# Two-layer graph network on one core: the Exp table load ahead of tile 0's count copies, an earlier credit, and y's split between the copies of the output weights

## The chip, the cores and the metric

The kernel runs on 1 core of a Trainium2 chip. TensorE (PE in the rows) multiplies into PSUM, VectorE (DVE) and ScalarE (ACT) work between PSUM and SBUF, GpSimd (POOL) only in SBUF, and SyncE (SP) issues most DMAs. Every engine takes its instructions in the order of its own program and waits on semaphores for the others. The metric is the device time of one execution in microseconds (us), lower is better; three executions of the kernel before are given.

## The reference

What is computed, cut to what matters here. N = 1250 nodes of 1024 numbers, 41,250 edges with one of two relations; the second layer's tables of counts come from the same edges.

```
h  = relu(layernorm(x))                       # 1250 x 1024
nx = t5_layer_norm(h, ln_weight)
out = nx @ W_root + bias                      # 1024 -> 286
for r in range(2):                            # relations
    msg  = nx[src] @ W_rel[r] * (edge_type == r)
    sums = segment_sum(msg, dst); cnt = segment_sum(edge_type == r, dst)
    out += sums / max(cnt, 1)
y  = elu(out) @ wo_weight                     # 286 -> 1024, the output weights
x1 = x + h + y
g  = relu(layernorm(x1)); hh = g @ W          # second layer, 1024 -> 1024
e  = exp(-leaky_relu(al[src] + ar[dst], 0.1))
out_x = x1 + elu(segment_sum(e * hh[dst], src) / (segment_sum(e, src) + 1e-5))
```

## The kernel before, in words

The nodes are 10 tiles of 125 rows. The sums over edges are done as dense products: for each tile of target nodes the kernel counts, by matmuls of one-hot rows, how many edges of each relation come from each source node, and multiplies that table of counts by the messages. A tile's counts are made in five groups of 25 target columns. There is no scheduler: the order on each engine is written out by hand, and the engines meet at semaphores.

- **First stage** (0 to 121 us): per tile, normalise, transpose, and multiply by the relation weights; ScalarE copies the result out as `msg_hi` (function `messages`, L545), VectorE writes the self term `root` (L951) and the low part `msg_lo` (L953). All products are done in high and low parts (hi*hi + hi*lo + lo*hi), so each operand exists as a rounded part and a remainder. Among the last tile's products TensorE also counts the five groups of target tile 0 (`windows_counted`, L1406), and ScalarE copies each into `adj0` (L579); five `zero_used` and five `zero_out` signals pace this. Then `back_to_exp` (L582) loads ScalarE's table with Exp and runs one tiny Exp, after which the last tile's `messages` follows.
- **Counting stage** (121 to 243 us): step t counts the groups of tile t (`counted`), copies them out (`counts_evicted`, L602 and L606: a float copy, then a 16-bit copy), multiplies tile t-1's counts by the messages (`summed`, L1502: relation 0 and relation 1 of 20 matmuls each), transposes the summed counts for the second layer in three parts (`turned`, L1526, copied out at L622), and finishes tile t-2: z (`z_of`, L1059 to L1065), its exponential (`elu`, L627), y (`y_of`, L1069 and L1071), its transpose (L1541, L1542), y's split into high and low (`y_split`: L635 on ScalarE, L1077 and L1080 on VectorE), and the output product (`output1`, L1558 to L1561, added to x at L1088). VectorE builds the one-hot rows for the counting (`rows_of`, L973 and L975, about 1.3 us for a group).
- The **output weights** are split once, in step 2: ScalarE copies `wo_hi` for two blocks of 127 rows (L610) and `wo_mix` for the rest (L616), VectorE subtracts (L1050 twice, L1054) and signals `wo_split`. TensorE's `output1(0)` waits for `wo_split` to reach 3, so for all of them; y's low part it needs too, and the middle part of the transposed counts, `turned(1, 1)`, waits for y's split because both use PSUM bank 5:

```
pe.wait_ge(S["yT_lo_rdy"], data(t))
pe.wait_ge(S["wo_split"], len(FK))     # len(FK) is 3
```

- **Credits.** Many semaphores start at 2 so that the first two tiles find their buffers free. VectorE gives `sum_16` its two credits at L1039, in its program behind the last tile's messages and the load of a flag; the first group of a tile's counts is not copied out by ScalarE before `sum_16` allows it (`act.wait_ge(S["sum_16"], room(t))`).
- Both sides of a branch are in the program; the flag says that all edges were found, and in the profiled execution the written-out order of `If_eq(flag, 0)` runs. The other side uses `split_wo` as a whole.
- **Second layer** (243 us to the end): products with W and the attention sums, on TensorE almost without a break.

Of the kernel before, what the change touches and what calls it, by code (L numbers as in the profile page):

```python
# [5 lines left out]
def rgcn_gat_kernel(nc, x, src, dst, edge_type, ln_weight, w_rel, w_root, conv_bias, wo_weight, w_gat, a_gat, out):  # L6

    F32, R32, BF16, F16 = mybir.dt.float32, mybir.dt.float32r, mybir.dt.bfloat16, mybir.dt.float16
    I32, U16 = mybir.dt.int32, mybir.dt.uint16
    ALU, ACT, AX = mybir.AluOpType, mybir.ActivationFunctionType, mybir.AxisListType.X  # L10
# [5 lines left out]
    T = 125  # L16
# [39 lines left out]
    CREDIT = 2  # L56
# [58 lines left out]
    with ctx:  # L115
# [9 lines left out]
        eps = sb(ctx, "eps", [P, 3], F32)  # L125
# [4 lines left out]
        ssq = [sb(ctx, f"ssq{b}", [T, 1], F32) for b in range(2)]  # L130
# [131 lines left out]
        S = {n: sem(n) for n in names}  # L262
# [224 lines left out]
        def _(act):  # L487
            A = nc.scalar
# [85 lines left out]
            messages(1, 1, 0)  # L574
            pads()
            pipeline((transposed, 1), (messages, 2), (normed, -1), steps=(AHEAD, TILES + 1))
            for g in range(NG):
                act.wait_ge(S["zero_used"], g + 1)
                A.copy(adj0[:, :, GW * WD * g:GW * WD * (g + 1)].rearrange("p r (n d) -> p r n d", d=WD), counts_bank(g)).then_inc(S["zero_out"], 1)  # L579

            def back_to_exp():
                A.activation(ssq[0][:], eps[0:T, 0:1], ACT.Exp)  # L582
            back_to_exp()
            messages(TILES - 1, 1, TILES // 2 - 1)
            act.wait_ge(S["zero_out"], NG)
            act.wait_ge(S["table_rdy"], 1)
# [19 lines left out]
                    A.copy(whole(adj_16), whole(adj_hi).bitcast(F32)).then_inc(S["win_16"], 1)  # L606

            def split_wo_of(n):
                    act.wait_ge(S["wo_in"][n], 32)
                    A.copy(wo_hi[:, n, :], wo_raw[:, n, :]).then_inc(S["wo_hi_rdy"], 1)  # L610

            def split_wo():
                split_wo_of(0)
                split_wo_of(1)
                act.wait_ge(S["wo_in"][2], 48)
                A.copy(wo_mix[:], wo_rest[:]).then_inc(S["wo_hi_rdy"], 1)  # L616

            def counts_out(t, b, d, parts=range(3)):
                for c in parts:
# [101 lines left out]
            with act.If_eq(flag, 0):  # L721
                act.wait_ge(S["g_ps"], data(TILES - 1))
                A.copy(ident_16[:], ident[:]).then_inc(S["ident_rdy"], 1)
                act.sem_inc(S["win_out"], NG)
                act.sem_inc(S["win_16"], NG)
                tile = lambda t: (t, t % 2, t // 2)

                def evicted(t, *groups):
                    for g in groups:
                        counts_evicted(t, t % 2, g, True)  # L730

                def turned(t, *parts):
                    counts_out(*tile(t), parts)
                evicted(1, 0, 1)
                turned(0, 0)
                evicted(1, 2)
                turned(0, 1)
                evicted(1, 3)
                turned(0, 2)
                evicted(1, 4)  # L740
                elu(*tile(0))
                evicted(2, 0)
                split_wo()
                evicted(2, 1)
                y_split(*tile(0))
                turned(1, 0)
                evicted(2, 2)
                turned(1, 1)
                evicted(2, 3)
                turned(1, 2)  # L750
                evicted(2, 4)
                elu(*tile(1))
                for t in range(3, TILES):
                    evicted(t, 0)
                    y_split(*tile(t - 2))
                    evicted(t, 1)
                    turned(t - 1, 0)
                    evicted(t, 2)
                    elu(*tile(t - 1))
                    turned(t - 1, 1)  # L760
                    evicted(t, 3)
                    turned(t - 1, 2)
                    evicted(t, 4)
                last = tile(TILES - 1)
                deviation2(0, 0)
                deviation2(1, 1)
                act.wait_ge(S["hot_used"], done(nth(TILES - 1, NG - 1)))
                split_gat_weights(range(0, 1))
                for k in range(1, 4):
                    load_wg(k)  # L770
                y_split(*tile(TILES - 2))
                norm2(0, 0)
                back_to_exp()
                for k in range(4, 6):
                    load_wg(k)
                turned(TILES - 1, 0)
                load_wg(6)
                elu(*last)
                turned(TILES - 1, 1)
                turned(TILES - 1, 2)  # L780
                load_wg(7)
                y_split(*last, yT_hi2)
                transposed2(0, 0, 0)
                norm2(1, 1)
                split_gat_weights(range(1, 5))
                transposed2(1, 1, 0)
                split_gat_weights(range(5, KT))
                second_layer()
# [21 lines left out]
        def _(dve):  # L810
            V = nc.vector
            dve.sem_inc(S["hot_used"], NG)
            dve.sem_inc(S["win_lo"], NG)
            dve.sem_inc(S["x_used"], 1)
            for n in ("bn_rdy", "var_rdy", "rs_rdy", "rstd_rdy", "rms_rdy", "hT_lo_rdy", "g_dve", "deg_rdy", "inv_rdy", "z1_rdy",
                      "zz_rdy", "y_rdy", "yT_lo_rdy", "x1_rdy", "bn2_rdy", "mv2_rdy", "rs2_rdy", "rstd2_rdy", "gT_lo_rdy", "h_dve",
                      "att_u", "att_v", "att_p", "att_lo_rdy", "den_rdy", "rinv_rdy", "logit_rdy"):
                dve.sem_inc(S[n], CREDIT)
# [217 lines left out]
                    dve.wait_ge(S["c_ps"], 3 * room(t))  # L1036
                V.tensor_tensor(columns(adj_lo, b, g), counts_bank(NG * b + g), columns(adj_hi, b, g).bitcast(F32), ALU.subtract).then_inc(S["win_lo"], 1)

            dve.sem_inc(S["sum_16"], CREDIT)  # L1039

            def summed(t, b, d):
                mine = slice(T * b, T * (b + 1))
                dve.wait_ge(S["win_16"], done(nth(t, NG - 1)))
                dve.wait_ge(S["c_ps"], 3 * room1(t))
                V.tensor_tensor(sum_16[:], adj_16[:, 0:TILES, mine], adj_16[:, TILES:BLOCKS, mine], ALU.add).then_inc(S["sum_16"], 1)

            def split_wo():
                for n in range(2):
                    dve.wait_ge(S["wo_hi_rdy"], n + 1)
                    V.tensor_tensor(wo_lo[:, n, :], wo_raw[:, n, :], wo_hi[:, n, :].bitcast(F32),  # L1050
                                    ALU.subtract).then_inc(S["wo_split"], 1)
                dve.wait_ge(S["wo_hi_rdy"], 3)
                middle = slice(FR, 2 * FR)
                V.tensor_tensor(wo_mix[middle, :], wo_rest[middle, :], wo_mix[middle, :].bitcast(F32), ALU.subtract).then_inc(S["wo_split"], 1)  # L1054
# [187 lines left out]
            with dve.If_eq(flag, 0):  # L1242
                tile = lambda t: (t, t % 2, t // 2)

                def rows(t, *groups):
                    if t < TILES:
                        for g in groups:
                            rows_of(nth(t, g))
                dve.wait_ge(S["zero_out"], NG)
                both = adj0[:].bitcast(F32)  # L1250
                V.tensor_tensor(sum_16[:], both[:, 0:TILES], both[:, TILES:BLOCKS], ALU.add).then_inc(S["sum_16"], 1)
                rows(2, 0, 1, 2, 3)
                z_of(*tile(0))
                rows(2, 4)
                y_of(*tile(0))
                summed(*tile(1))
                split_wo()
                y_split(*tile(0))
                rows(3, 0)
                z_of(*tile(1))  # L1260
                y_of(*tile(1))
                rows(3, 1)
                for t in range(3, TILES):
                    summed(*tile(t - 1))
                    rows(t, 2)
                    y_split(*tile(t - 2))
                    output1(*tile(t - 3))
                    rows(t, 3)
                    z_of(*tile(t - 1))
                    rows(t, 4)  # L1270
                    y_of(*tile(t - 1))
                    rows(t + 1, 0, 1)
                last, before = tile(TILES - 1), tile(TILES - 2)
                variance2(0, 0)
                variance2(1, 1)
                summed(*last)
                deviation2(0, 0)
                deviation2(1, 1)
                output1(*tile(TILES - 3))
                y_split(*before)  # L1280
                split_gat_weights(range(0, 1))
                z_of(*last)
                y_of(*last)
                output_half(TILES - 2, 0, 0)
                y_split(*last, yT_hi2, yT_lo2)
                output_half(TILES - 2, 0, 1)
                transposed2(0, 0, 0)
                split_gat_weights(range(1, 5))
                output1(*last)
                split_gat_weights(range(5, 7))  # L1290
                variance2(2, 0)
                split_gat_weights(range(7, KT))
                deviation2(2, 0)
                transposed2(1, 1, 0)
                second_layer()
# [423 lines left out]
```

## Time and profile before

| | us |
|---|---|
| median of 3 runs | 511.51 (510.75 to 511.76) |
| the profiled execution | 510.68 |
| its span | 508.9 |
| TensorE busy | 491.3 (97%) |
| VectorE busy | 374.2 (74%) |
| ScalarE busy | 227.4 (45%) |
| TensorE's waits in 121 to 143 us, by the profile | 0.60, 0.78, 0.52 |

Times in the trace are us from the span's start. The profiled execution is 1.78 us longer than its span. Busy shares are means over stages: in the counting stage the engines follow each other through semaphores every few us, and what bounds it is read from who waited for whom there.

### The profile page before, as it was taken

The numbers are of one execution on the slowest core, as the hardware profiler recorded it, in microseconds if no ns is written. First come the engines' busy times: TensorE is split into PE (matmuls) and PEld (weight loads), VectorE is DVE, ScalarE is ACT, GpSimd is POOL, SyncE is SP. The second block draws the span as 40 slices with busy tenths as digits, with TensorE's granted clock in tenths as the row PEclk, the third lists the DMA queues.
The fourth block names the chain that finished last, engine by engine and source line by source line (L and its number), as shares of the span: only waits on it lengthen the run. The fifth ranks groups of instructions, "written<-read, shape, count | busy, mean of one in ns | idle before, by whom it ended". The sixth has DMA issues, their size and how long they took to land.

```text
span 508.9 us, 7733 instructions
## 1 busy us (share of the span) xinstructions
PE 491.3 (97%) x2953; PEld 422.4 (83%) x2953; DVE 374.2 (74%) x635; ACT 227.4 (45%) x382; POOL 74.9 (15%) x74
## 2 busy tenths in 40 slices
PE   3999999999899999999999999999999999999996
PEld 2889989988889998998788888888888878878785
DVE  4865885599989999997855555556598877777634
ACT  5755543416966666668632222334233323323211
POOL 1182313100000000000000000000083333322400
PEclk9999999999999999999999999999999999999999
DMA  9964264504013334248911111100032232222211
GB/s 254 234 196 129 81 190 127 145 15 114 1 42 109 96 98 147 82 124 300 309 45 42 40 42 43 38 1 0 1 81 82 87 95 62 81 82 81 81 44 44
DMA packets 22186, 49.15 MB, mean 97 GB/s; under 512 B 4798, under 2 KB 10709, under 8 KB 22018
## 3 DMA queue, kind: packets, MB, share of 16 engines
q1 hardware_dynamic: 20879, 44.66, 29.6%
q10 hardware_dynamic: 1008, 3.67, 2.1%
q8 instruction: 26, 0.43, 0.4%
q0 software_dynamic: 256, 0.26, 0.2%
q14 instruction: 17, 0.14, 0.1%
HBM read 33.05 MB, written 16.85 MB: 98 GB/s over the span
## 4 chain that ended last, share of the span: by engine, by line
PE 84%; DVE 7%; DMA 4%; ACT 3%; issue 1%; SPq 0%; ACTq 0%; DVEq 0%
PE ps L1337 11%; PE ps L1605 9%; PE ps L1607 9%; PE ps L1606 9%; PE ps L1502 7%; PE ps L1586 7%; PE ps L1587 7%; PE ps L1588 7%; PE ps L1406 4%; PE ps L1425 2%; DMA xt<-xh_scratch 2%; PE ps L1558 2%; PE ps L1560 1%; PE ps L1559 1%; PE ps L1572 1%; DMA x_scratch<-xt 1%
## 5 line engine op out<-in xcount | busy, mean ns | idle before, releaser
L1605 PE MATMUL ps<-h_hi,att_hi 125*125 125x512 f32 (+1 forms) x190 | 73.6, 387 | 0.0
L1606 PE MATMUL ps<-h_lo,att_hi 125*125 125x512 f32 (+1 forms) x190 | 72.6, 382 | 0.0
L1607 PE MATMUL ps<-h_hi,att_lo 125*125 125x512 f32 (+1 forms) x190 | 72.6, 382 | 0.0
L1586 PE MATMUL ps<-wg,gT_hi 128*125 128x512 f32 x160 | 63.8, 399 | 0.1
L1587 PE MATMUL ps<-wg,gT_hi 128*125 128x512 f32 x160 | 63.1, 395 | 0.0
L1588 PE MATMUL ps<-wg,gT_lo 128*125 128x512 f32 x160 | 63.1, 394 | 0.0
L1502 PE MATMUL ps<-msg_hi,adj_hi 125*125 125x288 f32 x180 | 50.3, 304 | 0.8 <-ACT adj_hi L602 0.8
L1502 PE MATMUL ps<-msg_lo,adj_hi 125*125 125x286 f32 x180 | 45.9, 295 | 0.0
L477 POOL TENSOR_TENSOR some<-first_att 125x625 f32<-125x625 f32 x1 | 2.4, 2441 | 273.3 <-DVE first_att L1162 273.3
L697 ACT ACTIVATE em<-ps,rinv 125x512 f32<-125x512 f32 (+1 forms) x21 | 14.0, 668 | 63.2 <-DVE hp L1208 63.2
L1607 PEld LDWEIGHTS ps<-h_hi,att_lo 125*125 125x125 f32 x190 | 35.3, 186 | 8.0
L1605 PEld LDWEIGHTS ps<-h_hi,att_hi 125*125 125x125 f32 x190 | 35.2, 185 | 7.9
L1606 PEld LDWEIGHTS ps<-h_lo,att_hi 125*125 125x125 f32 x190 | 35.2, 185 | 7.5
L1337 PE MATMUL ps<-w_hi,hT_hi 128*125 128x430 f32 x112 | 40.7, 363 | 0.4 <-DVE hT_lo L928 0.4
L1337 PE MATMUL ps<-w_hi,hT_lo 128*125 128x430 f32 x112 | 40.2, 359 | 0.0
L1337 PE MATMUL ps<-w_lo,hT_hi 128*125 128x430 f32 x112 | 40.0, 357 | 0.0
L1142 DVE CUSTOM_DVE_ANT_0 h_lo<-ps,a_b 125x1024 fp32r<-125x1024 f32 x20 | 24.5, 1224 | 20.0 <-PE ps L1588 19.7
L1586 PEld LDWEIGHTS ps<-wg,gT_hi 128*125 128x125 f32 x160 | 29.7, 186 | 7.5 <-DVE wg L1103 0.5
L1588 PEld LDWEIGHTS ps<-wg,gT_lo 128*125 128x125 f32 x160 | 29.7, 186 | 7.3
L1587 PEld LDWEIGHTS ps<-wg,gT_hi 128*125 128x125 f32 x160 | 29.7, 186 | 6.9
L1502 PEld LDWEIGHTS ps<-msg_hi,adj_hi 125*125 125x125 f32 x180 | 33.4, 186 | 1.2 <-ACT adj_hi L602 1.2
L674 ACT CAST h_hi<-ps 125x1024 fp32r<-125x1024 f32 x10 | 10.1, 1014 | 54.1 <-DVE dot L1142 54.1
(215 smaller groups left out, 1102.3 us busy)
## 6 DMA issues: line engine op xcount, KB each, us to landing
xt<-in_x SPq DMA_DIRECT2D x10, 448.0 KB
xh_scratch<-xt SPq DMA_DIRECT2D x10, 448.0 KB
xt<-xh_scratch SPq DMA_DIRECT2D x10, 448.0 KB
x_scratch<-xt SPq DMA_DIRECT2D x10, 448.0 KB
x1t<-x_scratch SPq DMA_DIRECT2D x10, 448.0 KB
xr<-x_scratch SPq DMA_DIRECT2D x10, 448.0 KB
out_x<-xr SPq DMA_DIRECT2D x19, 224.0 KB
wg_raw<-in_L_gnn_W ACTq DMA_DIRECT2D x7, 512.0 KB, 7.8
```

Source lines behind the costliest of these rows:

```text
L697: A.activation(em[b][:, first:end], heads(b, h, (first, end)), ACT.Exp, scale=rinv[b][:, 0:1]).then_inc(S["el_rdy"], 1)
L1142: V.tensor_tensor_reduce(out=halves(h_lo[:, TILES - 1, :]), in0=hps, in1=halves(a_b[:, s, :]), scale=1.0, scalar=0.0, op0=ALU.mult, op1=AL ...
L1337: last = M.matmul(out, lhsT, rhs, start=(n == 0), stop=(n == len(terms) - 1))
L1406: last = M.matmul(win_bank(n, x), srcs, wide, start=c == 0, stop=c == SLOTS - 1)
L1425: last = M.matmul(bank(2 + 2 * b + n, T, FB), lhsT[b][:, k, :], rhs[:, k, n, :], start=k == 0 and m == 0, stop=k == KT - 1 and m == 2)
L1502: last = M.matmul(*product, start=(s == 0 and n == 0), stop=(end and n == 1), skip_group_check=True)
L1586: M.matmul(to, hi, wg[k][:, 0, cut], start=n == 0, stop=False)
L1587: M.matmul(to, hi, wg[k][:, 1, cut], start=False, stop=False)
L1588: last = M.matmul(to, lo, wg[k][:, 0, cut], start=False, stop=n == KT - 1)
L1605: M.matmul(to, hi[:, s, :], h_hi[:, s, cut], start=s == 0, stop=False)
L1606: M.matmul(to, hi[:, s, :], h_lo[:, s, cut], start=False, stop=False)
L1607: return M.matmul(to, lo[:, s, :], h_hi[:, s, cut], start=False, stop=s == TILES - 1)
```

## The change

Three things change, all around the first two steps of the counting stage.

1. ScalarE: `back_to_exp()` stands ahead of the five copies into `adj0` instead of behind them.
2. VectorE: the two credits of `sum_16` are given at the start of its program, with the others.
3. ScalarE and VectorE, in step 2: the three copies (and subtractions) of the output weights are no longer one piece. On ScalarE the second block follows y's split, and the rest follows the copy of group 2 of tile 2's counts; on VectorE y's split stands behind the first subtraction.

```diff
             pipeline((transposed, 1), (messages, 2), (normed, -1), steps=(AHEAD, TILES + 1))
+            def back_to_exp():
+                A.activation(ssq[0][:], eps[0:T, 0:1], ACT.Exp)
+            back_to_exp()
             for g in range(NG):
                 act.wait_ge(S["zero_used"], g + 1)
                 A.copy(adj0[:, :, GW * WD * g:GW * WD * (g + 1)].rearrange("p r (n d) -> p r n d", d=WD), counts_bank(g)).then_inc(S["zero_out"], 1)
-
-            def back_to_exp():
-                A.activation(ssq[0][:], eps[0:T, 0:1], ACT.Exp)
-            back_to_exp()
             messages(TILES - 1, 1, TILES // 2 - 1)
...
@@ ScalarE, the written-out order
                 evicted(2, 0)
-                split_wo()
+                split_wo_of(0)
                 evicted(2, 1)
                 y_split(*tile(0))
+                split_wo_of(1)
                 turned(1, 0)
                 evicted(2, 2)
+                split_wo_rest()
                 turned(1, 1)
                 evicted(2, 3)
...
@@ VectorE, start of its program
             dve.sem_inc(S["x_used"], 1)
+            dve.sem_inc(S["sum_16"], CREDIT)
...
-            dve.sem_inc(S["sum_16"], CREDIT)
-
...
@@ VectorE, the written-out order
                 summed(*tile(1))
-                split_wo()
+                split_wo_of(0)
                 y_split(*tile(0))
+                split_wo_of(1)
+                split_wo_rest()
                 rows(3, 0)
```

`split_wo_of(n)` and `split_wo_rest()` are the old parts of `split_wo()`, which now calls them in the old order.

ScalarE at the end of the first stage, before (L545 is `messages`, L579 the copies of tile 0's counts, L286 the flag):

```order
L529 CAST hT_hi<-ps 128x500 x2
L545 ACTIVATE msg_hi<-ps,stats 125x2x286
L579 CAST adj<-ps 125x20x25 x5
L582 ACT_TABLE_LOAD
L582 ACTIVATE ssq<-eps 125x1
L545 ACTIVATE msg_hi<-ps,stats 125x2x286
L286 TENSOR_LOAD table
```

and now (line numbers are those of the changed kernel):

```order
L529 CAST hT_hi<-ps 128x500 x2
L545 ACTIVATE msg_hi<-ps,stats 125x2x286
L578 ACT_TABLE_LOAD
L578 ACTIVATE ssq<-eps 125x1
L582 CAST adj<-ps 125x20x25 x5
L545 ACTIVATE msg_hi<-ps,stats 125x2x286
L286 TENSOR_LOAD table
```

The table load and the small Exp moved ahead of the five copies; the last tile's `messages` now follows the fifth copy.

ScalarE in step 2, before (L602 and L606 copy one group of counts, L610 and L616 the output weights, L635 y's split, L622 the transposed counts):

```order
L627 ACTIVATE eb<-zb,eps 125x286
L602 CAST adj_hi<-ps 125x20x25
L606 CAST adj<-adj_hi 125x20x25
L610 CAST wo_hi<-wo_raw 127x1024 x2
L616 CAST wo_mix<-wo_rest 96x1024
L602 CAST adj_hi<-ps 125x20x25
L606 CAST adj<-adj_hi 125x20x25
L635 ACTIVATE yT_hi<-ps 127x125 x2
L635 ACTIVATE yT_hi<-ps 96x125
L622 CAST counts<-ps 125x500
L602 CAST adj_hi<-ps 125x20x25
L606 CAST adj<-adj_hi 125x20x25
```

and now (L601 and L605, L609 and L613, L637, L624 are the same operations):

```order
L601 CAST adj_hi<-ps 125x20x25
L605 CAST adj<-adj_hi 125x20x25
L609 CAST wo_hi<-wo_raw 127x1024
L601 CAST adj_hi<-ps 125x20x25
L605 CAST adj<-adj_hi 125x20x25
L637 ACTIVATE yT_hi<-ps 127x125 x2
L637 ACTIVATE yT_hi<-ps 96x125
L609 CAST wo_hi<-wo_raw 127x1024
L624 CAST counts<-ps 125x500
L601 CAST adj_hi<-ps 125x20x25
L605 CAST adj<-adj_hi 125x20x25
L613 CAST wo_mix<-wo_rest 96x1024
```

y's split moved ahead of two of the three weight copies, and the last of these moved behind three more waits on TensorE's work: group 1, `turned(1, 0)` and group 2 of tile 2.

VectorE in the same step, now (L1048 is the sum of tile 1's counts at its head, L1052 and L1063 the subtractions, L1086 and L1089 y's split, L978 and L980 the one-hot rows of tile 3's group 0, L1068 the start of tile 1's z):

```order
L1048 TENSOR_TENSOR sum<-adj 125x1250
L1052 TENSOR_TENSOR wo_lo<-wo_raw,wo_hi 127x1024
L1086 SCALAR_TENSOR_TENSOR yT_lo<-ps,yT_hi 127x125 x2
L1089 SCALAR_TENSOR_TENSOR yT_hi<-ps,yT_hi 32x125
L1052 TENSOR_TENSOR wo_lo<-wo_raw,wo_hi 127x1024
L1063 TENSOR_TENSOR wo_mix<-wo_rest,wo_mix 32x1024
L978 TENSOR_TENSOR ring<-wkey,iota 128x5x200
L980 TENSOR_TENSOR ring<-wkey,iota 128x5x256
L1068 TENSOR_SCALAR deg<-ps 125x2
```

Before, the three subtractions stood together ahead of y's split; the one-hot rows of tile 3 and the z of tile 1 stand behind all of it in both.

## Rows read from the trace of the kernel before

**Rows 1.** The page: busy us and share of two engines, and TensorE's granted clock.
```profile
PE 491.3 (97%) x2953; PEld 422.4 (83%) x2953; DVE 374.2 (74%) x635; ACT 227.4 (45%) x382; POOL 74.9 (15%) x74
PEclk9999999999999999999999999999999999999999
```

**Rows 2.** Timeline of ScalarE: start, us, engine, line, out<-in, idle and releaser.
```profile
108.17 0.74 ACT L545 ACTIVATE msg_hi<-ps,stats 125x572 fp32r<-125x572 f32 x1 [8.38 <-PE ps L1337]
...
111.25 0.59 ACT L579 CAST adj<-ps 125x500 fp32r<-125x500 f32 x1 [1.12 <-PE ps L1406]
...
119.94 1.28 ACT L582 ACT_TABLE_LOAD   x1
...
121.34 0.72 ACT L545 ACTIVATE msg_hi<-ps,stats 125x572 fp32r<-125x572 f32 x1
...
122.83 0.59 ACT L602 CAST adj_hi<-ps 125x500 fp32r<-125x500 f32 x1 [0.58 <-DVEq L1039]
```

**Rows 3.** Timeline of SyncE's queue, at the end of the first stage.
```profile
120.56 1.69 SPq L292 DMA_DIRECT2D wo_raw<-in_L_gnn_wo_weight  x4
```

**Rows 4.** Timeline of VectorE, 122 to 131 us.
```profile
122.10 0.52 DVE L951 SCALAR_TENSOR_TENSOR root<-ps,stats,bias_b 125x286 f32<-125x286 f32 x1 [1.27 <-ACT msg_hi L545]
...
130.31 0.52 DVE L1063 SCALAR_TENSOR_TENSOR zb<-ps,deg,root 125x286 f32<-125x286 f32 x1
```

**Rows 5.** Timeline of TensorE, 124 to 144 us.
```profile
124.76 0.44 PE L1526 MATMUL ps<-ident,sum 125*125 125x126 f16 x4 [0.60 <-DVE sum L1251]
...
130.92 0.36 PE L1502 MATMUL ps<-msg_hi,adj_hi 125*125 125x288 f32 x1 [0.78 <-ACT adj_hi L602]
...
133.65 0.63 PE L1406 MATMUL ps<-ring_more 128*128 128x100 bf16 x10
...
137.40 0.62 PE L1406 MATMUL ps<-ring 128*128 128x100 bf16 x10
138.54 0.44 PE L1526 MATMUL ps<-ident,sum 125*125 125x126 f16 x4 [0.52 <-DVE yT_hi L1080]
...
139.85 0.47 PE L1558 MATMUL ps<-wo_hi,yT_hi 127*125 127x512 f32 x1
...
143.68 0.45 PE L1541 MATMUL ps<-ident,yb 125*127 125x125 f32 x2
```

**Rows 6.** Timeline of ScalarE, 132 to 143 us.
```profile
132.99 1.99 ACT L610 CAST wo_hi<-wo_raw 127x1024 fp32r<-127x1024 f32 x2
134.88 1.05 ACT L616 CAST wo_mix<-wo_rest 96x1024 fp32r<-96x1024 f32 x1
135.84 0.57 ACT L602 CAST adj_hi<-ps 125x500 fp32r<-125x500 f32 x1
136.44 0.63 ACT L606 CAST adj<-adj_hi 125x500 f16<-125x500 f32 x1
136.98 0.59 ACT L635 ACTIVATE yT_hi<-ps 127x125 fp32r<-127x125 f32 x3
...
142.27 0.53 ACT L627 ACTIVATE eb<-zb,eps 125x286 f32<-125x286 f32 x1
```

**Rows 7.** Timeline of VectorE, 136 to 143 us.
```profile
136.46 1.22 DVE L1054 TENSOR_TENSOR wo_mix<-wo_rest,wo_mix 32x1024 fp32r<-32x1024 f32 x1
...
138.52 0.68 DVE L973 TENSOR_TENSOR ring<-wkey,iota 128x1000 bf16<-128x1000 f16 x1
...
140.91 0.52 DVE L1065 SCALAR_TENSOR_TENSOR zb<-ps,deg,zb 125x286 f32<-125x286 f32 x1
142.83 0.46 DVE L1069 SCALAR_TENSOR_TENSOR yb<-eb,zb 125x286 f32<-125x286 f32 x1 [1.40 <-ACT eb L627]
```

**Rows 8.** Busy us of each engine by stretch: stretch, length, PE, PEld, DVE, ACT, POOL, clock.
```profile
132.00:138.00 6.00, 6.00 (x61) 5.80 (x59) 5.80 (x9) 5.90 (x11) 0.00 (x0) 1.00 0.00 1
156.00:168.00 12.00, 12.00 (x119) 11.03 (x118) 11.05 (x22) 8.11 (x18) 0.00 (x0) 1.00 0.28 85
```

**Rows 9.** Timeline of VectorE in the next step but one.
```profile
162.15 0.16 DVE L1059 TENSOR_SCALAR deg<-ps 125x2 f32<-125x2 f32 x1 [0.80 <-PE ps L1502]
```

More of the change, by code:

```diff
@@ L608, in split_wo_of, with split_wo_rest @@
             def split_wo_of(n):
-                    act.wait_ge(S["wo_in"][n], 32)
-                    A.copy(wo_hi[:, n, :], wo_raw[:, n, :]).then_inc(S["wo_hi_rdy"], 1)
+                act.wait_ge(S["wo_in"][n], 32)
+                A.copy(wo_hi[:, n, :], wo_raw[:, n, :]).then_inc(S["wo_hi_rdy"], 1)
+            def split_wo_rest():
+                act.wait_ge(S["wo_in"][2], 48)
+                A.copy(wo_mix[:], wo_rest[:]).then_inc(S["wo_hi_rdy"], 1)
             def split_wo():
@@ L614, in split_wo @@
                 split_wo_of(1)
-                act.wait_ge(S["wo_in"][2], 48)
-                A.copy(wo_mix[:], wo_rest[:]).then_inc(S["wo_hi_rdy"], 1)
+                split_wo_rest()
             def counts_out(t, b, d, parts=range(3)):
@@ L1045, in summed, with split_wo_of, split_wo_rest @@
                 V.tensor_tensor(sum_16[:], adj_16[:, 0:TILES, mine], adj_16[:, TILES:BLOCKS, mine], ALU.add).then_inc(S["sum_16"], 1)
+            def split_wo_of(n):
+                dve.wait_ge(S["wo_hi_rdy"], n + 1)
+                V.tensor_tensor(wo_lo[:, n, :], wo_raw[:, n, :], wo_hi[:, n, :].bitcast(F32),
+                                ALU.subtract).then_inc(S["wo_split"], 1)
             def split_wo():
[L1048 to L1051, printed above, removed]
+                split_wo_of(0)
+                split_wo_of(1)
+                split_wo_rest()
+            def split_wo_rest():
                 dve.wait_ge(S["wo_hi_rdy"], 3)
@@ L1256, in _ @@
                 summed(*tile(1))
-                split_wo()
+                split_wo_of(0)
                 y_split(*tile(0))
+                split_wo_of(1)
+                split_wo_rest()
                 rows(3, 0)
```

## The prediction

> **What bounds the kernel now.** First the page: TensorE is busy 97% of the span at a granted clock of 9 in all slices, ScalarE 45% [rows 1]. So the time is TensorE's instruction stream plus its few waits, and a change of order on other engines acts only through those waits. Next the timelines of the three engines around the change. TensorE waits three times between 121 and 143 us: 0.60 us for the summed counts of tile 0, 0.78 us ahead of tile 1's product, 0.52 us for y's split of tile 0 [rows 5]. From 138.54 on it runs through, and a whole later stretch of 12 us shows it busy for 12.00 [rows 8]: what it loses or wins up to there is kept, because it has no idle time to give back and all later transfers start from its progress. Last the busy time by stretch: from 132 to 138 us ScalarE is busy 5.90 of 6.00 us and VectorE 5.80 [rows 8]. In step 2, where the output weights are split, both are full, and this is the stretch the third edit reorders.
>
> **Edit 1, the table load.** Tile 9's `msg_hi` starts at 121.34, right behind the table load of 1.28 us (119.94) [rows 2]. Its input was ready earlier: SyncE's next DMA waits for the same semaphore and was issued at 120.56 [rows 3]. With the load gone from there it starts at 120.56, so 0.78 us earlier. The load and the small Exp now stand behind `messages` of tile 8, which ends at 108.91: 108.91 + 1.28 + 0.20 (the Exp; the distance 119.94 to 121.34 is 1.40 in all) is 110.3 to 110.4. The first copy into `adj0` slips by some 0.8 us to there, and ends at 110.99; the second waits for TensorE until 111.25 anyway [rows 2]. TensorE needs the first copy only for its third group (L1406 waits for `zero_out` from there on), which comes after the second. Cost 0; the cover is TensorE's products between the groups.
>
> What follows `msg_hi`: VectorE's `root` waited 1.27 us for it at 122.10 [rows 4] and starts at 121.32. Its messages, the sum of tile 0's counts, the one-hot rows and z of tile 0 stand behind it without a gap, so all move by 0.78. The first wait of TensorE (0.60 to the modelled end of the matmul before, some 0.75 from start to start) is for that sum and goes. The second is put down to ScalarE's copy, but the product waits for the first z operation of tile 0 as well, since it reuses the same PSUM banks, and that ended at 130.31 + 0.52 = 130.83 and TensorE started at 130.92, 0.09 behind it [rows 4, 5]. I take it that VectorE paces this, and the start moves from 130.92 to 130.14: the wait stays nearly as long, the shift is 0.78. Were it the copy after all, it would move by the 0.75 of the first wait, which is the other bound. I take **-0.78**; bounds -0.7 and -0.8 from this, and 0 if something else holds `msg_hi` (a rival).
>
> **Edit 2, the credit.** ScalarE's first copy out of tile 1 waited 0.58 us for it, until 122.83 [rows 2]. Now it can start about 121.6. But its next customer is TensorE, whose groups come later than the copies, and it is ahead of TensorE then. Even with the credit in its old place it would come 0.78 sooner through edit 1. Value 0, bounds 0 and -0.1.
>
> **Edit 3, y's split between the weight copies.** All times now in the new frame (before minus 0.78). ScalarE: the first weight copy at 132.99 - 0.78 = 132.21, half of the pair's distance of 1.89, so free at 133.16 [rows 6]. Now comes group 1 of tile 2, which waits for TensorE: 133.65 + 0.63 - 0.78 = 133.50 [rows 5], start 133.54, its two copies take 0.60 + 0.54 (135.84 to 136.44 to 136.98 [rows 6]), so y's split starts at 134.70 and ends 0.59 later at 135.29. VectorE's part of y takes 0.84 (the end of L1054 at 137.68 to the start of the rows at 138.52 [rows 7]): y's low part is ready at 136.15. TensorE wants it behind group 2 of tile 2, 137.40 - 0.78 = 136.62 plus 0.46 for the group, at 137.08. So **the third wait goes**, and TensorE has 138.54 - 137.08 = 1.46 us in hand.
>
> It then does two parts of the transposed counts and two groups, 139.85 - 138.54 = 1.31 [rows 5], and reaches `output1(0)` at 138.39. That waits for all three weight parts. ScalarE: second block 135.32 to 136.3; the copy of `turned(1, 0)` behind it is short and over by then; group 2 waits for TensorE's group 2, 137.40 + 0.62 - 0.78 = 137.24 [rows 5], so it starts at 137.30, and with 0.63 + 0.54 the rest's copy starts at **138.46** and ends 1.05 later at 139.51 [rows 6]. VectorE's subtraction waits for it, 139.54, takes 1.22 [rows 7] and signals at **140.76**. TensorE's output product starts at 140.80 where before it started at 139.85: it has stood 2.4 us. The shift is +0.95. Behind the waiting instruction on TensorE stand the output product and all of step 3; on VectorE, behind the waiting subtraction, stand the rows of tile 3 and the z of tile 1.
>
> The last piece is that second queue. VectorE's rows of tile 3 move from 138.52 to 140.77. From there to the end of z it is 140.91 + 0.52 - 138.52 = 2.91 [rows 7]: 143.68. ScalarE's exponential (0.53) is free to start at once and ends at 144.24, y follows at 144.27 where before it was 142.83, and takes 0.60; TensorE's transpose of y of tile 1 starts at 144.90. By its own stream it would be there at 140.80 + (143.68 - 139.85) = 144.63 [rows 5], so it waits 0.27 more. Shift 144.90 - 143.68 = **+1.22**. VectorE is then 1.44 late; before, it had its first idle time of 0.80 two steps on, at 162.15 [rows 9], so it catches up with the shifted TensorE there. The one-hot rows of the groups in step 3 come a few tenths before TensorE needs them; up to 0.2 may be lost on them. Bounds of the sum: +0.9 (if y of tile 1 is not late) to +1.7.
>
> **The sum.** -0.78 + 0 + (0.95 + 0.78) + 0.27 = +1.22. Against the profiled execution, 510.68 + 1.22 = 511.9 (span 508.9 to 510.1). That execution is 0.83 below the median of the runs, so in their measure 511.51 + 1.22 = 512.7. A change under 0.2%, here 1.02 us, can hardly be told from none, and this is just above it.
>
> The Trainium skill ("Perfetto Trace Analysis", "Identifying the Most-Contended Engine") says that for VectorE and ScalarE the share of time they execute tells how contended they are, and that the engine with the highest share is to be optimised first. By that ScalarE at 45% would not matter, every wait that TensorE loses would be won, and the time would be the first rival's. Here the trace disagrees with the mean: in the six us that are reordered ScalarE is at 98% [rows 8].
>
> **Rivals.**
> *Faster: the weight copies are never waited for.* The three waits of TensorE go or shrink and nothing comes in their place: -1.46, 510.05 in the runs' measure. It decides at one point: VectorE's third subtraction has to be done by 138.39, so the rest's copy has to start by 136.1 on ScalarE. For it: the weights' transfers were issued from 120.56 on [rows 3], and before the change ScalarE copied them in one go with the subtraction done at 137.68 [rows 7]. Against it: the copy now stands behind group 2, whose matmuls end at 137.24, and nothing passes on that engine. Break even is an output product at 139.85. Chance 0.08.
> *The table load was not what held `msg_hi`.* Then edit 1 gives nothing, and edit 3 costs 1.73 + 0.27 = 2.0: 513.5. For it: ScalarE's queue loads the flag in that same us. Against it: `msg_hi` starts 0.12 after the load's end, and VectorE had idled 1.27 for it [rows 2, 4]. Chance 0.08.
> *The loss is partly given back.* At the end of the counting stage the chain runs through two transfers and VectorE; if these have fixed times of their own, or if VectorE's late start of z costs nothing at TensorE, +0.3 to +0.9 is left, 512.1. Against it: each transfer there is started by an addition that follows TensorE's output product, so it moves along. Chance 0.14.
> *The clock.* TensorE stands for 2.4 us, three times as long as any wait in the middle of the trace. The granted clock is full in all slices, the first with its waits among them [rows 1], so I see no price; if it fell to 1.2 GHz for a few us, 2 to 4 us more, 515.7. Chance 0.03.
>
> **How the numbers follow.** The forecast (0.67, +0.9 to +1.7, with some 0.3 us of scatter in a median) lies above +1.02 in about two cases of three: 0.45. With the second rival (0.08) and the clock (0.03) and a little of the third (0.02), slower is 0.58. Within 0.2%: 0.22 of the forecast and 0.12 of the third rival, 0.34. Faster: the first rival, 0.08. The range leaves out that rival below and the clock above: 511.4 to 514.1; the likeliest case's own is 512.1 to 513.4.
>
> **What would show it.** The changed profile should have tile 9's `msg_hi` at 120.56, no wait at the first transposed counts, the product of tile 1 starting at 130.1, no wait at the second `turned`, then a wait of 2.4 us at the first `output1` put down to VectorE's `wo_mix` subtraction, which itself waited about 2.0 us for ScalarE's copy of the rest at 138.5; the first transpose of y of tile 1 at 144.9; and TensorE without a gap from there through steps 4 to 9. I am wrong if the first output product starts before 139.9, or if steps 4 to 9 run at another length than now.

## The result, and the profile after

| | before | changed |
|---|---|---|
| median | 511.51 us (5 runs, 510.75 to 512.82) | 513.73 us (5 runs, 513.19 to 514.48) |
| ratio | | 1.0042, 95% interval 1.003 to 1.0054 |
| span of the profiled execution | 508.9 | 511.4 |

The change makes the kernel 0.42% slower, 2.2 us; 512.7 was forecast. Two later comparisons of the same changed kernel gave 1.0048 (1.003 to 1.0066) and 1.0037 (1.0023 to 1.0051). Of all later executions one, of e1, took 2151.53 us, at full clock; its ratio leaves it out.

The first stage does not end at the same time in every execution (120.24 to 121.08 in the twelve profiles), which hides differences of tenths. So all places below are told as a distance from SyncE's DMA of the output weights [rows 3], which is issued on the last product's signal: 120.56 before, 120.94 after.

ScalarE's timeline after, the lines that answer to [rows 2]:

```profile
108.55 0.74 ACT L545 ACTIVATE msg_hi<-ps,stats 125x572 fp32r<-125x572 f32 x1 [8.38 <-PE ps L1348]
109.31 1.28 ACT L578 ACT_TABLE_LOAD   x1
...
110.71 0.57 ACT L582 CAST adj<-ps 125x500 fp32r<-125x500 f32 x1
111.63 0.59 ACT L582 CAST adj<-ps 125x500 fp32r<-125x500 f32 x1 [0.35 <-PE ps L1417]
...
120.95 0.74 ACT L545 ACTIVATE msg_hi<-ps,stats 125x572 fp32r<-125x572 f32 x1 [0.64 <-PE ps L1436]
```

The load lies in idle time, only the first copy slips (from 1.37 us behind the start of tile 8's `msg_hi`, 109.54 - 108.17, to 2.16), the second still waits for TensorE, and tile 9's `msg_hi` starts 0.01 us behind the signal instead of 0.78. TensorE's lines after, that answer to [rows 5]:

```profile
124.38 0.44 PE L1537 MATMUL ps<-ident,sum 125*125 125x126 f16 x4
...
130.55 0.37 PE L1513 MATMUL ps<-msg_hi,adj_hi 125*125 125x288 f32 x1 [0.78 <-ACT adj_hi L601]
...
137.49 0.40 PE L1537 MATMUL ps<-ident,sum 125*125 125x126 f16 x4
...
141.25 0.47 PE L1569 MATMUL ps<-wo_hi,yT_hi 127*125 127x512 f32 x1 [2.27 <-issue]
...
144.59 0.64 PE L1417 MATMUL ps<-ring 128*128 128x100 bf16 x10
145.34 0.48 PE L1552 MATMUL ps<-ident,yb 125*127 125x125 f32 x2
```

Two of the three waits before are gone and a new one of 2.27 us stands at the first output product. The transpose of tile 1's y starts 0.75 us behind the group ahead of it, where before it was 0.47 (143.68 - 143.21): it waits 0.28 for VectorE's y. The profile names no releaser ("issue"). The other engines' timelines do: ScalarE's, that answers to [rows 6], and VectorE's, that answers to [rows 7]:

```profile
138.33 0.64 ACT L605 CAST adj<-adj_hi 125x500 f16<-125x500 f32 x1
138.86 1.04 ACT L613 CAST wo_mix<-wo_rest 96x1024 fp32r<-96x1024 f32 x1
```

```profile
139.94 1.22 DVE L1063 TENSOR_TENSOR wo_mix<-wo_rest,wo_mix 32x1024 fp32r<-32x1024 f32 x1 [2.06 <-ACT wo_mix L613]
...
144.69 0.46 DVE L1078 SCALAR_TENSOR_TENSOR yb<-eb,zb 125x286 f32<-125x286 f32 x1 [0.60 <-ACT eb L629]
```

The rest's copy ends at 139.90, VectorE had idled 2.06 us for it, its subtraction ends at 141.16, and the output product starts at 141.25. So read, the new wait is the third weight part, which stands on ScalarE behind the copy of group 2.

### The profile page after: what moved, and what is told of

Its sections match the earlier page's. It is cut to its first block, busy times and chain, and to the rows that moved or that the text cites. A ratio compares the mean times of both kernels' runs of the same rounds, so it can differ in the third digit from the quotient of the medians.

```text
span 511.4 us, 7733 instructions
## 1 busy us (share of the span) xinstructions
PE 491.7 (96%) x2953; PEld 423.2 (83%) x2953; DVE 374.2 (73%) x635; ACT 227.8 (45%) x382; POOL 74.9 (15%) x74
## 4 chain that ended last, share of the span: by engine, by line
PE 86%; DVE 5%; DMA 4%; ACT 3%; issue 1%; SPq 0%; DVEq 0%
PE ps L1348 11%; PE ps L1513 10%; PE ps L1616 9%; PE ps L1618 9%; PE ps L1617 9%; PE ps L1597 7%; PE ps L1598 7%; PE ps L1599 7%; PE ps L1417 4%; PE ps L1436 2%; DMA xt<-xh_scratch 2%; DMA x_scratch<-xt 1%; PE ps L1583 1%; PE ps L1569 1%; PE ps L1398 1%; PE ps L1571 1%
```

## The experiments

Distances in us from the last product's signal, one profile each; the last column is the ratio to the kernel before in the comparison that belongs to it. The column "tile 9's transposed counts" is the last landmark in the counting stage; below it is called the stage's end.

| kernel | tile 9's msg_hi | tile 1's product | first output product | transpose of y, tile 1 | tile 9's transposed counts | ratio (95%) |
|---|---|---|---|---|---|---|
| before | 0.78 | 10.36 | 19.29 | 23.12 | 112.72 | |
| before, again (e5) | 0.80 | 10.37 | 19.30 | 23.13 | 112.72 | 0.9998 (0.9985 to 1.001) |
| changed | 0.01 | 9.61 | 20.31 | 24.40 | 114.06 | 1.0042 (1.003 to 1.0054) |
| changed, again (e4) | 0.00 | 9.60 | 20.32 | 24.41 | 114.06 | 1.0048 (1.003 to 1.0066) |
| changed, third (e6) | 0.01 | 9.60 | 20.30 | 25.55 | 115.19 | 1.0037 (1.0023 to 1.0051) |
| rest ahead (e1) | 0.01 | 9.61 | 18.28 | 22.40 | 112.02 | 0.9987 (0.9974 to 1.0001) |
| table load only (e2) | 0.00 | 9.60 | 18.54 | 22.38 | 111.97 | 0.9992 (0.9982 to 1.0002) |
| split only (e3) | 0.79 | 10.36 | 21.09 | 25.18 | 114.84 | 1.0054 (1.0039 to 1.007) |
| credit only (e7) | 0.78 | 10.36 | 19.29 | 23.12 | 112.71 | 0.9994 (0.9985 to 1.0003) |
| reordered (e8) | 0.00 | 9.60 | 17.86 | 21.69 | 111.31 | 0.9962 (0.9949 to 0.9975) |
| wait filled (e9) | 0.01 | 9.61 | 20.31 | 24.39 | 114.06 | 1.0022 (1.001 to 1.0033) |
| reordered, z sooner (e10) | 0.01 | 9.06 | 17.61 | 21.58 | 111.23 | 0.9973 (0.9957 to 0.9989) |

The landmarks of one kernel repeat within 0.02 us from one execution to the next, but for e6; the times of single runs of the kernel before spread over 2.4 to 4.0 us in one comparison.

**e1, the rest's copy moved ahead, one line.**

```diff
                 split_wo_of(1)
+                split_wo_rest()
                 turned(1, 0)
                 evicted(2, 2)
-                split_wo_rest()
                 turned(1, 1)
```

> The changed kernel with one instruction moved on ScalarE: the copy of the output weights' rest stands directly behind the second block, ahead of turned(1, 0) and group 2 of tile 2. Theory (the output product waits for this copy, which waits for group 2's matmuls): in a frame with tile 9's msg_hi at 120.56 the copy starts at 136.3, VectorE's subtraction is done at 138.8, TensorE's first output product starts at 138.8 instead of 140.8, the transpose of y of tile 1 at 143.1 instead of 144.9; against the kernel before -0.6 us, so 510.9 (ratio 0.9989). Rival (y's split between the copies costs by itself, by more switches and later subtractions, wherever the rest stands): the wait at the output product stays over 1.5 us and the time stays at 513 to 514. Rival (a fixed cost of the new order elsewhere, since 2.2 us were measured and 1.3 us are seen at step 3): it falls by 1.8 us only from what is seen, to about 512.

The output product came 2.03 us earlier than in the changed kernel and y of tile 1 2.00, and the stage stood 0.70 us under the kernel before; 0.9987 against 0.9989 expected. So the loss was this one copy behind group 2. The new order doesn't win anything either: e2 below has the same opening without the split, and its stage ends at 111.97 where e1's ends at 112.02. What e1 wins at y's split it gives back, for the output product still starts right behind VectorE's third subtraction, 18.28 behind the signal where e8 shows 17.86 without that wait. The timelines of ScalarE, with no wait between the second block and the copies of group 2, and of VectorE and TensorE:

```profile
135.53 1.05 ACT L609 CAST wo_hi<-wo_raw 127x1024 fp32r<-127x1024 f32 x1
136.46 1.06 ACT L613 CAST wo_mix<-wo_rest 96x1024 fp32r<-96x1024 f32 x1
137.41 0.58 ACT L624 CAST counts<-ps 125x500 uint16<-125x500 f32 x1
137.88 0.60 ACT L601 CAST adj_hi<-ps 125x500 fp32r<-125x500 f32 x1
...
137.86 1.22 DVE L1063 TENSOR_TENSOR wo_mix<-wo_rest,wo_mix 32x1024 fp32r<-32x1024 f32 x1
...
139.18 0.47 PE L1569 MATMUL ps<-wo_hi,yT_hi 127*125 127x512 f32 x1
```

**e2, the table load alone.**

```diff
+            def back_to_exp():
+                A.activation(ssq[0][:], eps[0:T, 0:1], ACT.Exp)
+            back_to_exp()
             for g in range(NG):
                 act.wait_ge(S["zero_used"], g + 1)
                 A.copy(adj0[...], counts_bank(g)).then_inc(S["zero_out"], 1)
-            def back_to_exp():
-                A.activation(ssq[0][:], eps[0:T, 0:1], ACT.Exp)
-            back_to_exp()
             messages(TILES - 1, 1, TILES // 2 - 1)
```

> The kernel before with the Exp table load and its small Exp ahead of tile 0's count copies, nothing else. Theory: tile 9's msg_hi starts 0.78 us earlier against SyncE's DMA of the output weights, the wait at the first transposed counts goes, tile 1's product and all behind it move by 0.75 to 0.78: 510.75, ratio 0.9985. The waits at y's split (0.5 us) stays. Rival (the gain is given back behind it, since ScalarE and VectorE are full up to 138 us): within 0.2 us of before. Rival (the table load ahead of the copies costs TensorE a wait for the first of them): slower by up to 0.8 us.

In the stage -0.76 at tile 1's product and -0.75 at its end: nothing is given back. The wait at y's split stays, 0.51 us. The medians, 0.9992 with an interval up to 1.0002, can't tell it from nothing.

**e3, the split alone.** The diff is the change's two pieces in step 2 ("the written-out order" of ScalarE and VectorE); table load and credit stand as before.

> The kernel before with the output weights' copies and y's split interleaved as in the change, table load and credit as before. Theory: no gain at the opening; first output product 1.73 us later than before, y of tile 1 0.27 more: +2.0 us in the counting stage, 513.5, and by what the change itself showed beyond the stage up to 0.8 more, so 513.5 to 514.3 (ratio 1.004 to 1.0055). Rival (the loss in the measured time comes from the opening edits, and the interleaving costs only what the stage shows in the change, 1.3 us): 512.8.

+1.80 at the output product, +2.12 at the stage's end, 1.0054. The loss belongs to the split, the opening gives back 0.78 of it. The ratio's 2.8 us are again more than the stage's 2.12. TensorE's wait is the same 2.27 us as in the changed kernel; the granted clock stayed at 1.00 behind it in the profiled execution.

**e4, the changed kernel again.** No edit.

> The changed kernel once more, on the same chip as its variants. In the profile of the first run the stage showed a shift of 1.35 us against the kernel before, the span 2.5 and the median 2.2. If the part beyond the stage is a property of the kernel (later transfers that meet others), the ratio is 1.004 again and the landmark shifts of the second layer stand over those of step 3 by 0.5 or more. If it is scatter of the first loads and of the last stores, the ratio comes out at 1.002 to 1.003 and the shift inside the counting stage is 1.35 again.

114.06 again, to 0.01. But six runs spread from 511.32 to 514.68, and the ratio stood at 1.0048: 2.4 us, where the stage shows 1.34. Neither of the two expected outcomes: inside the stage it repeated exactly, in the median it didn't come down.

**e5, the kernel before as its own rival.** No edit.

> The kernel before as its own rival, unchanged: it says how far an identical kernel lands from 1 in these comparisons, and gives a second profile. Expected ratio 1.000 with an interval of some 0.1 to 0.2% to each side; from the semaphore of the last product of the first stage (SyncE's DMA of the output weights) to the first transposed counts of the last tile 112.72 us as in the first profile, within 0.1. If the first stage ends at 120.8 to 121.0 here too, as it does in three of the changed kernels, the 0.2 to 0.4 us at the entry are scatter; if it ends at 120.56 again, they belong to the new order of the program.

0.9998, 112.72 again. The first stage ended at 121.08 here, so the tenths at the entry are scatter.

**e6, the changed kernel a third time.** No edit.

> The changed kernel a third time, beside a copy of the kernel before. Inside the counting stage +1.34 us against the kernel before, as in both profiles so far. If the 0.9 to 1.1 us that the medians show over this are real, the ratio is 1.004 to 1.005 once more; if they are scatter, 1.0025 to 1.003.

The ratio, 1.0037, lies between the two. The profile settled more than the ratio: here the stage took 1.13 us longer than in the two earlier profiles of the same program, all of it between the output product and the transpose of tile 1's y, 5.25 us further on. Its output product starts at the same 20.30; its first matmuls then come 0.43 us apart instead of 0.23:

```profile
141.16 0.76 PE L1569 MATMUL ps<-wo_hi,yT_hi 127*125 127x512 f32 x1 [2.26 <-issue]
141.72 0.63 PE L1570 MATMUL ps<-wo_lo,yT_hi 127*125 127x512 f32 x1
142.15 0.63 PE L1571 MATMUL ps<-wo_hi,yT_lo 127*125 127x512 f32 x1
...
144.54 0.39 PE L1570 MATMUL ps<-wo_lo,yT_hi 127*125 127x512 f32 x1
144.77 0.40 PE L1571 MATMUL ps<-wo_hi,yT_lo 127*125 127x512 f32 x1
```

Busy time and granted clock by stretch (stretch, length, PE, PEld, DVE, ACT, POOL, clock, DMA), the same execution and then the first profile of the changed kernel:

```profile
139.00:141.00 2.00, 0.00 (x0) 0.00 (x0) 1.16 (x1) 1.97 (x4) 0.00 (x0) 0.98 0.00 0
141.00:142.00 1.00, 0.84 (x2) 0.77 (x3) 0.97 (x3) 1.00 (x3) 0.00 (x0) 0.50 0.00 0
142.00:143.00 1.00, 1.00 (x3) 0.70 (x3) 0.90 (x4) 0.82 (x2) 0.00 (x0) 0.50 0.00 0
143.00:144.00 1.00, 1.00 (x4) 0.80 (x3) 0.96 (x2) 0.00 (x0) 0.00 (x0) 0.50 0.06 16
144.00:145.00 1.00, 1.00 (x5) 0.77 (x4) 0.40 (x2) 0.54 (x1) 0.00 (x0) 0.83 0.00 0
```

```profile
139.00:141.00 2.00, 0.00 (x0) 0.00 (x0) 1.06 (x1) 1.97 (x4) 0.00 (x0) 1.00 0.00 0
141.00:142.00 1.00, 0.75 (x3) 0.67 (x4) 0.97 (x3) 1.00 (x3) 0.00 (x0) 1.00 0.00 0
142.00:143.00 1.00, 1.00 (x6) 0.79 (x5) 0.92 (x3) 0.91 (x2) 0.00 (x0) 1.00 0.09 16
```

Behind the same wait the clock was at 0.50 of full speed, the 1.2 GHz level, in one execution and at 1.00 in the other. Four profiles have this wait, three of the changed kernel and that of e3, and one of the four shows the fall.

Each run also lists its mean clock over the whole span. It is a rough sign, because it takes in the end of the span too: in the profile of e5 (the kernel before, mean clock 0.996) the granted clock is 1.00 up to 503 us and falls only behind TensorE's last product, which starts at 503.90:

```profile
120.00:150.00 30.00, 28.10 (x283) 26.37 (x282) 26.77 (x48) 24.23 (x46) 0.00 (x0) 1.00 0.19 49
503.00:515.00 12.00, 1.18 (x10) 0.97 (x9) 1.33 (x3) 0.47 (x1) 0.00 (x0) 0.77 0.09 24
```

So 0.996 proves nothing. Eight of the 17 runs of the changed kernel, the profiled one of e6 among them, had a mean of 0.995 or lower, and so had one of the six runs of e3, but none of the 81 of the kernel before in the later comparisons. Two more of the 17 stood at 0.996, and one of the 81. The ten of the 17 at 0.996 or lower took 513.04 to 514.68 us with a mean of 513.9, the seven above 511.32 to 513.38 with a mean of 512.6.

**e7, the credit alone.**

```diff
             dve.sem_inc(S["x_used"], 1)
+            dve.sem_inc(S["sum_16"], CREDIT)
...
-            dve.sem_inc(S["sum_16"], CREDIT)
```

> The kernel before with the two credits of sum_16 given at the start of VectorE's program, nothing else. Theory: ScalarE's first copy out of tile 1 starts some 0.3 us earlier (right behind the small copy of ident at 122.2), TensorE needs none of it, 0 us: ratio 1.000. Rival (ScalarE, full from 131 us on, carries the gain to the output weights): up to 0.3 us faster. The landmarks of TensorE from the first transposed counts to tile 1's product stay where they are.

ScalarE's first copy out of tile 1 starts 1.59 us behind the signal instead of 2.27 (122.83 - 120.56), 0.68 sooner and so twice what was expected, and then waits 0.68 us for TensorE at the first transposed counts, where it had no wait before. Every landmark of TensorE stands where it was.

```profile
122.49 0.59 ACT L602 CAST adj_hi<-ps 125x500 fp32r<-125x500 f32 x1
...
125.57 0.57 ACT L622 CAST counts<-ps 125x500 uint16<-125x500 f32 x1 [0.68 <-PE ps L1525]
```

**e8, another order in step 2.**

```diff
@@ ScalarE
                 split_wo_of(0)
+                split_wo_of(1)
                 evicted(2, 1)
                 y_split(*tile(0))
-                split_wo_of(1)
+                split_wo_rest()
                 turned(1, 0)
                 evicted(2, 2)
-                split_wo_rest()
                 turned(1, 1)
                 evicted(2, 3)
                 turned(1, 2)
-                evicted(2, 4)
                 elu(*tile(1))
+                evicted(2, 4)
@@ VectorE
                 split_wo_of(0)
-                y_split(*tile(0))
                 split_wo_of(1)
+                y_split(*tile(0))
                 split_wo_rest()
```

> The changed kernel with another order in step 2. ScalarE: both big blocks of the output weights, then group 1 of tile 2, y's split, the rest, turned(1, 0), group 2, and the exponential of tile 1 ahead of group 4; VectorE: two subtractions, y's split, the third. Theory, in a frame with msg_hi at 120.56: the copies end at 134.1 and 136.8, VectorE signals y at 136.7 and the third weight part at 138.05, so that TensorE waits neither at turned(1, 1) (137.08) nor at the output product (138.39); y of tile 1 follows at 142.2: -1.4 us against the kernel before in the counting stage, 509.4 on this chip's level (ratio 0.9973). Rival (one of the two comes late by a few tenths): -1.0. Rival (the late copy of group 4 holds step 3): wait of up to 0.5 us at tile 3's counts.

As expected in the stage, -1.41, and 0.9962 in the ratio: faster than both kernels. The landmarks are the ones to trust here, since the interval reaches from -1.3 to -2.6 us.

**e9, the wait filled.**

```diff
                     if t == 2:
+                        for s in range(16):
+                            M.matmul(ps[0:T, 6, 0:FP], adj_hi[:, s, T:2 * T], msg_hi[:, s % TILES, 0, :], start=True, stop=True, skip_group_check=True)
                         output1(0)(*tile(0))
```

> The changed kernel with 16 extra products of tile 1's counts by messages on TensorE ahead of its first output product, in the time in which it waits for the third weight part (0.13 us each, 2.1 us in all, into the bank that the output product then starts anew; their results are thrown away). They need nothing that is not there, and the output product is not later by them. Theory (in about half of the executions the wait of 2.3 us lets the granted clock fall to 0.5 for some 3 us behind it, which costs 1.1 us more; in the others it does not): with the wait filled no execution shows a mean clock of 0.995 or less, the landmarks in the counting stage stand at +1.34 us, and the median falls from 1.0045 to about 1.0026, 512.2. Rival (the executions over 513.5 come from elsewhere, such as late transfers): 1.004 to 1.005 as before. Rival (the extra products cost time themselves): the output product starts later than 20.3 us behind the last product of the first stage.

The output product stands at 20.31, the stage at 114.06, so the extra products cost nothing and the loss of 1.34 is still there. The ratio fell to 1.0022, and none of 12 runs showed a mean clock under 0.998 (511.23 to 512.60 us). Two things keep this short of a proof. Its interval, 1.001 to 1.0033, overlaps those of the changed kernel, and e9 ran on another chip than e4 and e6, where the changed kernel without the extra products was not run beside it. TensorE's lines and the stretches of this kernel:

```profile
138.16 2.35 PE L1684 MATMUL ps<-msg_hi,adj_hi 125*125 125x288 f32 x16
140.61 0.47 PE L1569 MATMUL ps<-wo_hi,yT_hi 127*125 127x512 f32 x1
```

```profile
136.00:140.50 4.50, 4.50 (x59) 4.26 (x57) 2.43 (x2) 3.85 (x7) 0.00 (x0) 1.00 0.00 0
140.50:144.00 3.50, 3.40 (x16) 2.57 (x16) 2.78 (x7) 2.29 (x5) 0.00 (x0) 1.00 0.02 5
```

**e10, z of tile 0 ahead of a group's one-hot rows, on top of e8.**

```diff
-                rows(2, 0, 1, 2, 3)
+                rows(2, 0, 1, 2)
                 z_of(*tile(0))
-                rows(2, 4)
+                rows(2, 3, 4)
```

> The reordered version (e8) with one more move on VectorE: z of tile 0 stands ahead of the one-hot rows of tile 2's group 3. Theory (tile 1's product waits for VectorE's first z operation, not for ScalarE's copy to which the profile puts it down): with msg_hi at 120.56 z starts at 128.45 when relation 1's product is done, its first part ends at 129.35, and the product starts as soon as ScalarE's copy ends, 129.6 instead of 130.1; TensorE's wait of 0.78 us shrinks to about 0.25, all behind it moves 0.5 us: -1.9 us in the counting stage, ratio 0.995 to 0.996. Rival (ScalarE's copy is what it waits for): the product stays at 10.1 us behind the last product's signal.

The product of tile 1 came at 9.06, 0.54 sooner, and its wait shrank from 0.77 to 0.23 us, still put down to the same copy. That copy did not move: it ends 9.00 us behind the signal in e8 (129.47 + 0.59 - 121.06) and 9.01 in e10 (128.66 + 0.59 - 120.24). VectorE's first part of z did, from 9.50 to 8.76. ScalarE and VectorE in e8, then ScalarE, VectorE and TensorE in e10:

```profile
129.47 0.59 ACT L601 CAST adj_hi<-ps 125x500 fp32r<-125x500 f32 x1
130.04 0.52 DVE L1072 SCALAR_TENSOR_TENSOR zb<-ps,deg,root 125x286 f32<-125x286 f32 x1
...
128.66 0.59 ACT L601 CAST adj_hi<-ps 125x500 fp32r<-125x500 f32 x1
128.48 0.52 DVE L1072 SCALAR_TENSOR_TENSOR zb<-ps,deg,root 125x286 f32<-125x286 f32 x1
129.30 0.40 PE L1513 MATMUL ps<-msg_hi,adj_hi 125*125 125x288 f32 x1 [0.23 <-ACT adj_hi L601]
```

So VectorE paced it in e8, as the prediction read, and with z out of the way the copy does in e10. The rest of the expectation was a miss: of 0.54 only 0.11 was left at y of tile 1 and 0.08 at the stage's end (-1.49 for -1.9). It went at two transposes: that of tile 0's y now started 0.69 us behind group 1 where 0.47 is the distance without a wait, and that of tile 1's 3.97 us behind the output product instead of 3.83. Both wait for VectorE's y, and VectorE had the same work ahead of these as before. By these two waits it is VectorE that now holds step 2; no run tests that. The medians, 0.9973 here and 0.9962 in e8, don't tell the two apart.

## Why the prediction was right, and where it fell short

- **The table load, -0.78.** Right: -0.75 to -0.76 (e2, and the change itself). The prediction kept 0.75 for the case that ScalarE's copy paces tile 1's product; the size doesn't tell the two cases apart, since that copy and z both moved by 0.76 to 0.77. e10 does. The cover was there, and nothing held `msg_hi` in its place, so that rival fell.
- **Tile 1's product follows VectorE's z, not the copy that the profile names.** Right, by e10: the copy stood still there and the product moved.
- **The credit, 0.** Right for TensorE, by e7.
- **The wait for y's split goes.** Right: it was to start at 16.52 behind the signal (137.08 - 120.56) and did at 16.55.
- **The rest's copy behind group 2 holds the output product.** Right in mechanism and size: 20.24 forecast, 20.31 measured; e1 moves this one copy and takes 2.03 us back. y of tile 1 was forecast at 24.34 and came at 24.40. The shift at the stage's end was forecast as +1.22 and was +1.34; the 0.06 more between y of tile 1 and step 4 lies within the tenths allowed for the one-hot rows of step 3. Which of the waits there took it I did not separate. Nothing of the loss was given back by the stage's end, so the rival that expected it fell.
- **Most contended by busy share: the faster rival fell.** The rule in "Perfetto Trace Analysis", "Identifying the Most-Contended Engine" (the Trainium skill) goes by the share of time that an engine executes. Taken over the whole span, as the prediction took it, it puts ScalarE at 45%, yet a ScalarE copy held TensorE for 2.3 us here; the rows of six us decided.
- **The size failed by one term.** Measured 2.2 us against 1.2 forecast. The stage accounts for 1.34. The term that fits the rest is the clock, which the prediction held at a chance of 0.03 and let cost nothing in its sum: "The granted clock is full in all slices, the first with its waits among them [rows 1], so I see no price". By the mean clock it fell in eight to ten of 17 runs. Its price was also wrong, 1.15 us (25.55 - 24.40) instead of 2 to 4. Eight to ten in 17 of 1.15 is 0.5 to 0.7; with 1.34 that makes 1.9 to 2.0, inside all three intervals (1.5 to 2.8, 1.5 to 3.4 and 1.2 to 2.6 us). The fall and its price are shown in one profile, how often it comes is worked out from mean clocks. e9 speaks for the link: the same lateness with TensorE kept busy costs 0.22%, 1.1 us, and has no run at the low clock; what it leaves open is said there.
- **Why the argument for that chance was weak.** The trace of before had no wait of this length in its middle, and its first slice is no witness: there the granted clock is listed as 1.00, but two matmuls of 430 columns took 0.71 us from start to start at 11.75 and 0.40 at 17.74. At e6's pace behind the wait, 0.43 us for 512 columns at 0.50, two of 430 would take 0.72, so an estimate from these rows has the clock at half there too; no run shows what else may have held them. The page's digits are coarse, too: e6's fall turns one of the 40 from 9 to 8, and by the same measure (slices of 12.7 us, a 9 for 90% or more) one of under 2.5 us would turn none, an estimate.

```profile
11.75 0.92 PE L1384 MATMUL ps<-w_lo,hT_hi 128*125 128x430 f32 x2
12.46 0.92 PE L1387 MATMUL ps<-w_hi,hT_lo 128*125 128x430 f32 x2
...
17.74 0.56 PE L1384 MATMUL ps<-w_lo,hT_hi 128*125 128x430 f32 x2
18.14 0.55 PE L1387 MATMUL ps<-w_hi,hT_lo 128*125 128x430 f32 x2
```

What stays open: why the clock falls in some executions and not in others behind the same wait; whether the changed kernel falls to it as often on the chip of e9; and what each median holds beyond the stage and the clock, since the start of the second layer (TensorE waited 0 to 0.7 us there for VectorE's part of W) and the last stores differ between executions of one kernel by several tenths.

## What to carry to other kernels

When a copy is moved into a gap on an engine that looks idle on average, follow every wait that it is now queued behind, and follow it to the one instruction that needs all its parts: a wait for "all three" makes the last one the price of the whole. Price a new wait of TensorE twice, once for its length and once for the clock behind it, and look whether the trace has a wait of that length before calling the second free. Where an early stage scatters, measure landmarks from a signal next to the change: here they repeat to 0.02 us, while a ratio over a dozen runs is known to some 0.5 us to each side.

## What the runs showed of the hardware

- Behind a wait of 2.27 us in the middle of dense matmuls the granted clock was at 0.50 for about 3 us in one of four profiles (e6; it was 0.98 in the stretch of the wait itself and 1.00 again from 145 us; the other three stayed at 1.00), and the mean clocks put the fall in eight to ten of the 17 runs of the changed kernel. Behind waits up to 0.8 us in the same stage none of the other eight profiles shows it.
- The price was 1.15 us: seven 512-column matmuls came 0.43 us apart instead of 0.23, 1.4 us in all, of which 0.28 went into the wait for y of tile 1 that the other profiles have.
- With sixteen products in place of the wait the granted clock was 1.00 in the profiled execution (e9), and no mean clock of 12 runs was under 0.998.
- A wait that the profile puts down to one engine's copy was another's: moving VectorE's first z operation cut it from 0.77 to 0.23 us while the named copy stayed where it was (e8, e10).
